# A second bias by DMA and VectorE, and a third identity add on GpSimd, in a masked-mixing and per-sample-matmul kernel

## What is computed

```python
# stage 1: masked softmax over rows, whose result is added to x
attn_in = tanh(x @ W1 + b1)                     # (64, 128, 128)
scores = attn_in @ v                            # (64, 128)
masked = where(mask_of_type[j, l], scores[:, None, :], -1e30)
p = softmax(masked, axis=-1)
x = x + (p @ x) / count(mask, axis=-1)
# stage 2: each sample has its own category
out = x + x @ W[cat] + b[cat]
```

## Time and profile before

| what | value |
|---|---|
| time, median of 3 runs | 311.19 us (310.75 to 311.24) |
| time of the profiled execution | 310.89 us |
| its span, first to last instruction | 308.9 us |
| TensorE busy | 299.9 us, 97% of the span |
| VectorE busy | 281.9 us, 91% |
| ScalarE busy | 266.6 us, 86% |
| GpSimd busy | 90.1 us, 29% |
| granted TensorE clock | 0.999 of full speed |
| moved by DMA | 105.69 MB, mean 342 GB/s |

### The profile page before, as it was taken

The page is one execution under the profiler, slowest core; times in us unless marked ns, Lnnn a source line. Parts: engine busy times, 40 slices in busy tenths (PEclk is TensorE's granted clock), DMA queues, the critical chain, the costliest instruction groups (busy, mean ns, idle before and its releaser), DMA issues.

```text
span 308.9 us, 4918 instructions
## 1 busy us (share of the span) xinstructions
PE 299.9 (97%) x1292; PEld 233.8 (76%) x1292; DVE 281.9 (91%) x383; ACT 266.6 (86%) x431; POOL 90.1 (29%) x123
## 2 busy tenths in 40 slices
PE   7999899899999999999999999999999999999995
PEld 4444686688787878878788887878888787888884
DVE  4459889999999999999999999999999999999961
ACT  2287988989999998999999899998989999899952
POOL 4011612334142243414224341322434132302100
PEclk9999999999999999999999999999999999999999
DMA  7999999999999999999999999999999999997243
GB/s 265 366 426 366 421 412 423 371 344 326 360 372 332 396 313 405 356 356 375 337 404 300 407 363 363 365 337 398 311 405 355 353 380 308 413 333 228 66 135 137
DMA packets 23516, 105.69 MB, mean 342 GB/s; under 512 B 2625, under 2 KB 2626, under 8 KB 13378
## 3 DMA queue, kind: packets, MB, share of 16 engines
q1 hardware_dynamic: 23202, 104.08, 90.6%
q10 hardware_dynamic: 288, 1.31, 1.1%
HBM read 88.61 MB, written 16.78 MB: 341 GB/s over the span
## 4 chain that ended last, share of the span: by engine, by line
PE 82%; DMA 6%; issue 5%; DVE 3%; ACT 1%; POOL 1%; ACTq 0%; POOLq 0%; SPq 0%; DVEq 0%
PE ps_y L653 16%; PE ps_y L655 16%; PE ps_y L654 16%; PE ps_pre L615 12%; DMA w_raw<-in_L_cond_W 6%; PE ps_y L665 4%; PE ps_y L666 4%; PE ps_y L667 4%; PE ps_y L671 3%; PE ps_pT L632 2%; PE ps_y L641 1%; PE ps_scores L625 1%; PE ps_scores L623 1%; POOL w_raw L274 1%; DVE w_lo L465 1%
## 5 line engine op out<-in xcount | busy, mean ns | idle before, releaser
L465 DVE TENSOR_TENSOR w_lo<-w_raw,w_hi 128x2048 fp32r<-128x2048 f32 x60 | 140.1, 2335 | 0.0
L336 ACT ACTIVATE w_hi<-w_raw 128x2048 fp32r<-128x2048 f32 x60 | 115.5, 1924 | 8.9 <-POOL w_raw L274 7.5
L653 PE MATMUL ps_y<-w_hi,xT_hi 128*128 128x512 f32 x240 | 95.0, 396 | 0.0
L655 PE MATMUL ps_y<-w_hi,xT_lo 128*128 128x512 f32 x240 | 93.6, 390 | 0.0
L654 PE MATMUL ps_y<-w_lo,xT_hi 128*128 128x512 f32 x240 | 93.4, 389 | 0.0
L274 POOL TENSOR_TENSOR w_raw<-w_raw,ident 128x512 f32<-128x512 f32 x30 | 39.2, 1307 | 132.6 <-DVE w_lo L465 82.6
L655 PEld LDWEIGHTS ps_y<-w_hi,xT_lo 128*128 128x128 f32 x240 | 45.0, 188 | 9.8
L654 PEld LDWEIGHTS ps_y<-w_lo,xT_hi 128*128 128x128 f32 x240 | 45.1, 188 | 9.1
L653 PEld LDWEIGHTS ps_y<-w_hi,xT_hi 128*128 128x128 f32 x240 | 45.1, 188 | 8.9 <-issue 0.2
L493 DVE TENSOR_TENSOR z_lo<-ps_y,z_hi 128x512 fp32r<-128x512 f32 x64 | 43.5, 680 | 5.4 <-ACT z_hi L372 5.3
L372 ACT ACTIVATE z_hi<-ps_y 128x512 fp32r<-128x512 f32 x64 | 38.7, 604 | 7.8 <-PE ps_y L655 5.1
(11 more groups left out here) (70 smaller groups left out, 352.8 us busy)
## 6 DMA issues: line engine op xcount, KB each, us to landing
w_raw<-in_L_cond_W SPq DMA_DIRECT2D x63, 1024.0 KB, 8.6
out<-out_sb SPq DMA_DIRECT2D x64, 256.0 KB, 6.2
x_raw<-in_x SPq DMA_DIRECT2D x15, 1024.0 KB, 7.4
out_sb<-in_L_cond_b SPq DMA_DIRECT2D x16, 256.0 KB, 5.7
x_raw<-in_x SPq DMA_DIRECT2D x2, 512.0 KB, 4.8
w_raw<-in_L_cond_W ACTq DMA_DIRECT2D x1, 1024.0 KB, 6.1
w_pack<-in_W_b_v ACTq DMA_DIRECT2D x1, 257.0 KB, 2.9
b_raw<-in_L_cond_b SPq DMA_DIRECT2D x2, 128.0 KB, 12.9
```

The costliest lines, as they stand in the source:

```text
L336: nc.scalar.activation(w_hi[k % NH][:], w_raw[k % NW][:], ACT.Copy).then_inc(w_hi_ready, 1)
L465: nc.vector.tensor_tensor(w_lo[k % NL][:], w_raw[k % NW][:], w_hi[k % NH][:].bitcast(F32), ALU.subtract).then_inc(w_lo_ready, 1)
L653: nc.tensor.matmul(y[:], xT_hi[q][:, c, xs], w_hi[k % NH][:, c, :], start=(c == 0), stop=False)
L655: last = nc.tensor.matmul(y[:], xT_lo[q][:, c, xs], w_hi[k % NH][:, c, :], start=False, stop=(c == DC - 1))
```

## The change

`WIDE` becomes the pair (1, 3). Samples with k % 4 = 3 lose their bias matmul on TensorE and their copy on ScalarE; SP spreads their bias over `out_sb` by a DMA, and VectorE adds it. The bookkeeping of semaphores follows (`sum_count`, one `wide_in` for each place). `by_pool` now also names samples with k % 4 = 0 from k = 12 on: GpSimd adds the identity to thirteen W (samples 12, 16, ... 60) to which VectorE added it before.

```diff
-    WIDE = 1
+    WIDE = (1, 3)
 ...
         def by_pool(k):
-            return k > G and k % G in (1, 2)
+            return k > G and (k % G in (1, 2) or k % G == 0 and k > 2 * G)
 ...
         def wide(k):
-            return k % G == WIDE
+            return k % G in WIDE
 ...
-            def load_wide(g):
-                cat = sp.value_load(ids_row[0:1, G * g + WIDE:G * g + WIDE + 1], min_val=0, max_val=C - 1)
-                if g >= 1:
-                    sp.wait_ge(out_stored[WIDE], 16 * g)
-                sp.dma_start(out_sb[WIDE][:], bias[bass.ds(cat, 1), :].to_broadcast([P, D])).then_inc(wide_in, 16)
+            def load_wide(k):
+                cat = sp.value_load(ids_row[0:1, k:k + 1], min_val=0, max_val=C - 1)
+                if k >= NO:
+                    sp.wait_ge(out_stored[k % NO], 16 * (k // NO))
+                sp.dma_start(out_sb[k % NO][:], bias[bass.ds(cat, 1), :].to_broadcast([P, D])).then_inc(wide_in[k % G], 16)
 ...
             load_w(6)
-            load_wide(0)
+            load_wide(WIDE[0])
+            load_wide(WIDE[1])
 ...
                 if b == 2 and 1 <= g < GROUPS:
-                    load_wide(g)
+                    load_wide(G * g + WIDE[0])
+                if b == 0 and 2 <= g <= GROUPS:
+                    load_wide(G * (g - 1) + WIDE[1])
 ...
                 elif k % G == 2 and k - 2 > G:
                     pool.wait_ge(av_lo_ready, k // G + 1)
+                elif k % G == 0:
+                    pool.wait_ge(w_lo_ready, w_count(k - 2))
 ...
             for g in range(GROUPS):
+                if g >= 3:
+                    add_identity(G * g)
                 if g >= 1:
                     add_identity(G * g + 1)
                     add_identity(G * g + 2)
 ...
             tanh_group(2)
-            copy_out(3)
             split_w_hi(9)
 ...
             split_z_lo(5)
+            add_wide(WIDE[1])
             split_w_lo(8)
 ...
                 split_z_lo(k - 1)
-                if b == 0:
-                    add_wide(g - 1)
+                if wide(k - 3):
+                    add_wide(k - 3)
                 if k + 4 < B and not by_pool(k + 4):
                     add_identity(k + 4)
 ...
+            add_wide(B - 1)
```

More of the change, by code:

```diff
@@ L171, in program @@
         sum_ready = sem("sum_ready")
-        wide_in = sem("wide_in")
+        wide_in = [sem(f"wide_in{i}") for i in range(G)]
         block = ctx.enter_context(nc.Block())
@@ L185, in by_pool, with sum_count @@
         def by_pool(k):
-            return k > G and k % G in (1, 2)
+            return k > G and (k % G in (1, 2) or k % G == 0 and k > 2 * G)
         def pool_count(k):
-            return max(k // G - 1, 0) * 2 + (min(k % G, 2) if k > G else 0)
-        assert all(pool_count(k) == sum(by_pool(i) for i in range(k + 1)) for k in range(B))
+            return sum(by_pool(i) for i in range(k + 1))
         def wide(k):
-            return k % G == WIDE
+            return k % G in WIDE
+        def sum_count(k):
+            return sum(wide(i) for i in range(k + 1))
         def wait_out(engine, k):
             if wide(k):
-                engine.wait_ge(sum_ready, k // G + 1)
+                engine.wait_ge(sum_ready, sum_count(k))
             else:
-                engine.wait_ge(out_ready, k - (k + G - WIDE - 1) // G + 1)
+                engine.wait_ge(out_ready, k + 1 - sum_count(k))
         @block.sync
@@ L494, in split_z_lo, with add_wide @@
                                         ALU.subtract).then_inc(z_lo_ready, 1)
-            def add_wide(g):
-                k = G * g + WIDE
+            def add_wide(k):
                 dve.wait_ge(pz_done, k + 1)
-                dve.wait_ge(wide_in, 16 * (g + 1))
-                nc.vector.tensor_tensor(out_sb[WIDE][:], ps_y[k % NY][:], out_sb[WIDE][:], ALU.add)\
+                dve.wait_ge(wide_in[k % G], 16 * (k // G + 1))
+                nc.vector.tensor_tensor(out_sb[k % NO][:], ps_y[k % NY][:], out_sb[k % NO][:], ALU.add)\
                     .then_inc(sum_ready, 1)
@@ L562, in _ @@
             add_identity(7)
-            add_wide(0)
+            add_wide(WIDE[0])
             split_w_lo(6)
```

## The result

The changed kernel takes 320.38 us (median of 6 runs, 319.17 to 321.41) against 311.15 us (6 runs, 310.74 to 312.95) for the kernel before: a ratio of 1.0283, 95% interval 1.0259 to 1.0308. The forecast was 316.1 us, slower; the time lies inside the range (310.4 to 320.9), near its upper end. The sign came out as said, but of +9.2 us only +4.9 were forecast. Medians and ratios are of the fast runs; one slow run, of e3_pool, is left out.

What follows compares the result with a forecast made beforehand. TensorE was taken as the bound at 18.13 us a group, then VectorE at 18.57: 12 x 0.44 = 5.3, -0.16 + 0.5 - 0.3 - 0.4, in all +4.9, so 316.1 us by the median; range 310.4 to 320.9.

Steps and rivals of the forecast that it cites:

- the hold: In steady groups GpSimd's third add, behind mask copies, overlaps VectorE's xT_lo and lengthens it by 0.70 us (0.60 to 0.91).
- the small terms: Per group on VectorE: 0.10 us wait before the reciprocal, 0.05 for a mask copy holding w_lo; bias add fills 0.24 wait.
- the tail: End of the program: bias matmuls of samples 59 and 63 are gone, -0.4 us.
- Queued behind it are the next W loads ...: nothing: SP's queue in steady groups: the added bias load and the store waiting for VectorE delay later W loads at no cost.
- the steady part: Repeating groups: twelve at +0.44 us each give 5.3, the last group -0.16, TensorE's lag -0.3.
- the lag of TensorE: From the end of av_lo to the scores' second matmul: used up first once VectorE is the bound, -0.3 us.
- the ramp: Start of the program: sample 3's bias add and the extra bias load cost +0.5 us, between 0 and 0.6.
- The slack list: VectorE's waits per group before the change: 0.24 us for TensorE's scores and 0.17 for GpSimd's row_div, leaving 17.72 of work.
- The hidden hold: Rival: in steady groups the hold is absent or hidden, VectorE 17.72 and TensorE 17.90 us a group; 308.3 us, 12%.
- the small hold: Rival: mask copies come early, overlap near 0.3 us costs 0.2, a group takes about 18.05; 310.4 to 312 us, 7%.
- the lost race: Rival: xT_lo begins before GpSimd's add, which then holds the next w_lo for 1.17 us; 321.7 us, 6%.
- The DMA queue as the bound: Rival: loads bound the steady group, the extra 0.26 MB making it 18.49 us; about 316 us, 4%.

Runs made afterwards that it cites:

- e3_pool: Kernel before with only GpSimd's third identity add, biases as before: 314.56 us, ratio 1.0157.
- e2_masks: Changed kernel, with GpSimd copying the masks before row_div, a group earlier, so nothing stands ahead of the third add: 317.42 us, ratio 1.0208.
- e9_early: e5_both with group 0's biases all by matmul and GpSimd's first two adds of a group released before the w_lo they waited for ends: 306.52 us, ratio 0.9831.
- e1_tail: Changed kernel, with SP issuing the bias load of sample 4g + 3 ahead of the store of sample 4g + 1: 316.15 us, ratio 1.0147.
- e6_pool_masks: e3_pool with the mask copies moved as in e2_masks, biases as in the kernel before: 309.89 us, ratio 0.9931.
- e5_both: Changed kernel with the edits of both e1_tail and e2_masks: 312.41 us, ratio 1.0039.
- e11_after: The changed kernel run once more, unaltered, to look at its start: 322.39 us in one execution.
- e4_bias: Changed kernel with the third identity add back on VectorE, leaving the second bias alone: 321.12 us, ratio 1.03.

## Why the prediction was right, and where it was wrong

**Right: the hold.** Its place, its cause and its size came from the overlaps in the rows of before, and the runs bear out all three. The add was to begin 0.70 us after `w_lo`, and begins after 0.68; the price taken was 0.70 and is 0.65. The group came to 18.51 us against 18.57, and e2_masks, which moves only the four copies ahead of the add, takes 0.44 of it away. The Trainium skill, SBUF — State Buffer, section "Who interferes with whom", has a loser that blocks fully; the trace agrees but for the 0.13 us that again are missing from the price, and e9_early agrees with its sentence that the order of issue decides who blocks.

**Right: the small terms.** The reciprocal waits 0.16 us in the group shown (166.37 to 167.13, of which the add takes 0.60); from the first held group on it waits some 0.17 in nine groups and not at all in four, 0.12 in the mean, and 0.10 was taken. The bias add fills the wait ahead of the maximum, as said.

**Mis-sized by 4.05 us: the tail.** The forecast gave the tail -0.4 for the bias matmuls gone; it is +3.65. The failed step is "Queued behind it are the next W loads ...: nothing". It asked what stands behind the new load on SP, and only in the steady group. It never asked what the load itself stands behind, a store that waits for VectorE, and what that costs where no later group covers it. The program's order showed it: `load_wide` of sample 63 comes after the store of sample 61 in the same pass of the loop. e1_tail shows it to be that place alone. With this step done right, 316.1 + 4.05 would have been 320.1. The prediction's own sign of being wrong, that VectorE waits for loads, came true here. That the time still lies in the range is luck in part: the upper bound of 320.9 was made for a larger hold, and no term of it allowed for a wait in the tail.

**Mis-sized: the steady part, by 0.8 us.** Eleven places have the full hold, not twelve: in the first, `xT_lo` takes 2.68 us and the group is 0.19 shorter than before. In the eleven a group is 0.38 us longer than before, not 0.44, which makes some 0.65 us. The other way, the last group comes to 18.10 where 17.97 was worked out; `xT_lo` takes 2.48 us there, 0.20 too long where 0.15 was allowed. And the lag of TensorE that was to give 0.3 wasn't used up: from the end of `av_lo` to the scores' second matmul pass 0.31 to 0.36 us in the groups of both kernels.

**Mis-sized: the ramp.** +0.5 was taken. From the first reciprocal on it is +0.31 in the two executions of the table and +1.1 in the mean of all (between nothing and 1.7). The rest of the +1.80 is the start, which varies by 1.03 us in the kernel before. The steady part's -0.8 and the ramp's +1.3 partly cancel, which is luck too.

**Wrong place: where TensorE waits.** The prediction has it wait for `av_lo` at the scores. It waits for `xT_lo` at the hidden layer, in the profile after (waits: engine, line, releaser, us in total, times, longest; then the place in the group shown, from TensorE's timeline):

```profile
PE ps_pre L624 <- issue: 6.2, 12, 0.7
```

```profile
172.74 0.39 PE L676 MATMUL ps_y<-z_lo,mix_hi 128*128 128x512 f32 x1
173.65 0.47 PE L624 MATMUL ps_pre<-xT_hi,w_hi 128*128 128x512 f32 x1 [0.52 <-issue]
```

The view names no releaser. But the program has the hidden layer wait for `xT_lo`, and in each of the twelve places it starts 0.10 us after `xT_lo` ends (here 173.55).

**Incomplete: the bound before.** "TensorE sets the pace" came from a busy share of 100%. e3_pool and e6_pool_masks show that the group was as long as the loop through the hidden layer and `xT_lo`, of which TensorE's own work is 17.98 us. The slack list had the two waits of VectorE, but not that delaying `xT_lo` is paid at once. For the change as a whole VectorE's sum hid the mistake, since it was the longer of the two: in the groups of the changed kernel VectorE no longer waits ahead of the maximum. The 17.90 us for TensorE was too high for the same reason: 17.98 - 0.23 is 17.75, and e9_early runs a group in 17.73.

**Rivals.** The hidden and the small hold fell with the 2.93 us of `xT_lo`, the lost race with the add that begins first. The DMA queue as the bound fell with e2_masks and e5_both, whose usual groups move the same bytes in 18.06 to 18.07 us; single bias adds did wait for their loads in steady groups, 0.3 to 0.7 us in e2_masks and in e11_after and 2.38 once in e4_bias. The hidden hold was worked out at 308.3 us. With the add put right, the queue mended and group 0 left alone the change gives 306.5, but e9_early also takes away the 0.19 us hold of the kernel before, which that rival kept.

## What to carry to other kernels

When work goes to an engine that can hold up the bound one, look at what each of its instructions overlaps, and let it arrive while the other is busy rather than just after: waiting in line cost the helper time that it had, and the bound engine nothing. For every DMA that is added, ask what it stands behind in its queue and which engine the instruction ahead of it waits for, in the last iteration above all. A 100% busy engine may still stand in a loop with another one; take the time between the releasing and the released instruction before calling it the bound.

## What the hardware showed that was not expected

- Small GpSimd instructions are held as large ones are: `row_div` took 0.76 us under a VectorE identity add, where 0.20 is its time in e2_masks without one, and three mask copies 2.47 us under a `w_lo`. The `row_div` of 166.34 begins 0.02 us ahead of the identity add in the records and is held all the same; who goes first can't be told from starts that are so close.
- A GpSimd add that arrives during a `w_lo` is served as soon as it ends and finishes 1.16 us after that (162.19 to 163.35), with no mark on VectorE; one that begins 0.68 us after the start of the `z_lo` that follows costs VectorE 0.65 us.
- The first reciprocal of one and the same program came at 17.06 and at 18.09 us. Two executions that are compared stage by stage should be compared from after the first loads on.
